# The context's rounding remainder: one instruction on GpSimd, or three on VectorE behind the pieces of the transposed remainder

## The reference

```
x: (32, 56, 160)    ctx_768: (32, 1500, 96)
x = L0(x, ctx)      attention to 3 x 16 context rows, 8 heads, w_out, + x
x = L1(x, ctx)      self-attention 20 heads of 64; cross-attention to all 1500 keys, 20 heads; GEGLU
x = L2(x, ctx)      cross-attention to 1496 keys, 8 heads, + a small attention over 4 tokens
x = L3(x, ctx)      self-attention 20 heads of 8; cross-attention to 1500 keys, 20 heads; GEGLU

cross-attention:  q = LN(x) @ wq ; k = ctx @ wk ; v = ctx @ wv
                  softmax(q k^T * scale) v ; @ wo + bo ; + x
```

## Time and profile before

| | us |
|---|---|
| median of 3 runs | 6753.15 |
| lowest, highest | 6720.8, 6789.24 |
| the profiled execution | 6721.46 |
| its span in the profile | 6719.7 |
| PE busy | 6012.4 (89%) |
| ACT, POOL, DVE busy | 3118.8 (46%), 3022.3 (45%), 2824.2 (42%) |
| mean granted clock of PE | 0.913 of full speed |

### The profile page before, as it was taken

How to read it: one execution, slowest core, us unless ns; L and a number is a source line. 1 busy time by engine, 2 the same in 40 slices (tenths; PEclk the granted TensorE clock), 3 DMA queues, 4 the chain that set the end, 5 groups by cost and what they waited for, 6 DMA issues and landing times.

```text
span 6719.7 us, 107050 instructions
## 1 busy us (share of the span) xinstructions
PE 6012.4 (89%) x34384; PEld 4911.2 (73%) x34384; DVE 2824.2 (42%) x4978; ACT 3118.8 (46%) x7280; POOL 3022.3 (45%) x2992
## 2 busy tenths in 40 slices
PE   7999999999999999998888887999989888888888
PEld 5777777777777777775666665677777777777776
DVE  2444443443433433433555544444444444444442
ACT  1444444444444444453444443345554555454554
POOL 0344444444444444452454544344554554455454
PEclk8899998898999999987999998789998999998998
DMA  2000000000000000000111111000000000000000
GB/s 54 11 14 15 10 14 15 12 14 14 14 15 8 14 14 15 11 18 19 26 27 26 25 26 29 11 18 14 14 17 18 14 14 14 15 17 14 18 14 9
DMA packets 84450, 114.90 MB, mean 17 GB/s; under 512 B 42814, under 2 KB 64682, under 8 KB 83978
## 3 DMA queue, kind: packets, MB, share of 16 engines
q1 hardware_dynamic: 83978, 108.56, 5.9%
HBM read 104.06 MB, written 4.46 MB: 16 GB/s over the span
## 4 chain that ended last, share of the span: by engine, by line
PE 66%; issue 11%; DVE 8%; ACT 7%; POOL 5%; DMA 2%; ACTq 0%; POOLq 0%; DVEq 0%; SPq 0%
PE ps_c L681 14%; PE ps_c L1061 6%; PE ps_u L1134 6%; PE ps_s L1119 5%; PE ps_s L1121 5%; PE ps_s L1120 5%; PE ps_u L1135 5%; PE ps_u L1136 5%; POOL p_lo L1587 4%; PE ps_c L1080 3%; ACT p_hi L1800 2%; ACT p L1798 1%; PE ps_c L861 1%; PE ps_c L1101 1%; PE ps_c L887 1%
## 5 line engine op out<-in xcount | busy, mean ns | idle before, releaser
L1587 POOL TENSOR_TENSOR p_lo<-p,p_hi 125x448 fp32r<-125x448 f32 (+2 forms) x2688 | 2717.8, 1021 | 3078.6 <-ACT p_hi L1800 2898.8
L1798 ACT ACTIVATE p<-ps_s 125x448 f32<-125x448 f32 (+2 forms) x2688 | 1321.1, 491 | 2330.0 <-PE ps_s L1121 2046.4
L1437 DVE TENSOR_REDUCE mpiece<-ps_c 125x1 f32<-125x500 f32 (+1 forms) x1984 | 1270.6, 672 | 320.1 <-PE ps_c L1061 301.4
L1800 ACT ACTIVATE p_hi<-ps_s 125x448 fp32r<-125x448 f32 (+2 forms) x2688 | 1315.9, 490 | 0.0
L1134 PE MATMUL ps_u<-p_hi,ctx_hi 125*97 125x448 f32 (+2 forms) x2688 | 1023.8, 381 | 171.7 <-POOL p_lo L1587 167.2
L1119 PE MATMUL ps_s<-q_hi,ctxT_hi 105*125 105x448 f32 (+3 forms) x2688 | 1023.7, 381 | 162.4 <-issue 84.9
L1120 PE MATMUL ps_s<-q_lo,ctxT_hi 96*125 96x448 f32 (+2 forms) x2688 | 951.2, 354 | 0.0
L1121 PE MATMUL ps_s<-q_hi,ctxT_lo 96*125 96x448 f32 (+2 forms) x2688 | 948.4, 353 | 0.0
L1135 PE MATMUL ps_u<-p_hi,ctx_lo 125*96 125x448 f32 (+2 forms) x2688 | 944.3, 351 | 0.0
L1136 PE MATMUL ps_u<-p_lo,ctx_hi 125*97 125x448 f32 (+2 forms) x2688 | 942.0, 350 | 0.0
L1061 PE MATMUL ps_c<-ctxT_hi,q_hi 96*125 96x500 f32 (+1 forms) x2112 | 863.1, 421 | 64.7 <-DVE mpiece L1437 23.0
(11 more groups left out here) (231 smaller groups left out, 5960.9 us busy)
## 6 DMA issues: line engine op xcount, KB each, us to landing
ctx_raw<-in_ctx SPq DMA_DIRECT2D x96, 562.5 KB
pT<-recs SPq DMA_DIRECT2D x32, 420.0 KB, 3.4
w_area<-recs SPq DMA_DIRECT2D x32, 420.0 KB, 3.4
w_area<-recs SPq DMA_DIRECT2D x32, 168.0 KB, 3.4
cs<-in_ctx SPq DMA_DIRECT2D x192, 6.0 KB, 2.8
x_between<-x_out SPq DMA_DIRECT2D x32, 80.0 KB
x_in<-x_between SPq DMA_DIRECT2D x32, 80.0 KB
w_area<-in_L_xattn_wq SPq DMA_DIRECT2D x2, 800.0 KB, 5.7
```

The lines of the kernel that those rows point to most:

```text
L1437: z = V.tensor_reduce(mpiece[0:wide, k, r:r + 1], C(0, wide, n % banks(t), 0, PIECE), AX.X, ALU.max)
L1587: P.tensor_tensor(p_lo[0:kp, k % 3, 0:w], p32[0:kp, k % 2, 0:w], p_hi[0:kp, k % 3, 0:w].bitcast(F32), ALU.subtract).then_inc(*sig("pl_ready"))
L1798: A(p32[0:kp, k % 2, 0:w], ps_s[0:kp, k % 2, 0:w], ACT.Exp, scale=DH[t.ph] ** -0.5)
L1800: A(p_hi[0:kp, k % 3, 0:w], ps_s[0:kp, k % 2, 0:w], ACT.Exp, scale=DH[t.ph] ** -0.5)\
```

## The change

`ctx_lo` is no longer made by POOL in one instruction of 1152 columns, but by DVE in three of 384 columns, each behind the piece of `ctxT_lo` of the same number. Its semaphore counts three per context instead of one, and SP and PE wait for the third. POOL's part `context` is gone.

```diff
-    "ctx_hi": ((2, 2, 2), 0), "ctx_lo": ((2, 2, 2), 1),
+    "ctx_hi": ((2, 2, 2), 0), "ctx_lo": ((6, 6, 6), 1),
...
             def load_context(t, b):
 
-                sp.wait_ge(*got("ctx_lo", t, b))
+                sp.wait_ge(*got("ctx_lo", t, NPIECE * b))
...
                         pe.wait_ge(*got("mr_ready", t, b + 1))
-                        pe.wait_ge(*got("ctx_lo", t, b + 1))
+                        pe.wait_ge(*got("ctx_lo", t, NPIECE * (b + 1)))
...
                         V.tensor_tensor(ctxT_lo[:, b, k], C(0, DC, r % banks(t), 0, PIECE), ctxT_hi[0:DC, b, k].bitcast(F32),
                                         ALU.subtract).then_inc(*sig("ctl_ready"))
+                        if r == 0:
+                            dve.wait_ge(*got("ctx_hi", t, b + 1))
+                        c = slice(4 * r, 4 * r + 4)
+                        V.tensor_tensor(ctx_lo[:, b, c, :], ctx_raw[:, 4 * DC * r:4 * DC * r + 4 * DC].rearrange("p (c d) -> p c d", c=4),
+                                        ctx_hi[:, b, c, 0:DC].bitcast(F32), ALU.subtract).then_inc(*sig("ctx_lo"))
...
-                @staticmethod
-                def context(t, b):
-
-                    yield 2
-                    pool.wait_ge(*got("ctx_hi", t, b + 1))
-                    P.tensor_tensor(ctx_lo[:, b, :, :], ctx_raw[:, :].rearrange("p (c d) -> p c d", c=NC),
-                                    ctx_hi[:, b, :, 0:DC].bitcast(F32), ALU.subtract).then_inc(*sig("ctx_lo"))
```

## The result

| | before | changed kernel |
|---|---|---|
| median, 20 runs each | 6767.64 us | 6793.76 us |
| lowest, highest | 6698.78, 6822.67 | 6768.51, 6841.44 |
| ratio to before, 95% interval | | 1.0058 (1.0035 to 1.0081) |
| span of the profiled execution, granted clock | 6719.7 us, 0.913 | 6798.1 us, 0.908 |

The ratios leave out the few runs of the kernel before that were in a slower state, and are not the quotients of the medians (here 1.0039).

A forecast was written before the change was run, and what follows sets the result against it. It took PE, busy 89% of the span, as the bound. Six places summed to 3.0 us, times 15 is +45 us; on the 6753.15 us median that gave 6798, rounded to 6795 us, range 6665 to 6880.

The forecast's parts named there:

- Sum and sign: Whole kernel: six kinds of place, 15 times each, sum to +45 us, slower, at 6795 us.
- Price of a piece: DVE's 384-column subtraction: 0.55 us bare, up to 1.7 beside a p_lo; median 0.6 to 0.9; three take 2.2 to 2.8.
- Phase 1, first, 0: First context, phase 1: POOL's wait replaced by a 0.95 us longer wait for ctxT_lo; 0 us, bounds -0.5 to +0.4.
- my own rule: On DVE: a piece that meets a running p_lo of POOL waits for its end.
- Phase 1, second, +1.7: Second context, phase 1: reciprocal 3 us late delays line 1464 and the maximum; +1.7 us, bounds 1.0 to 3.3.
- Phase 2, first, +0.4: First context, phase 2: two pieces ahead of the third correction partly fit DVE's waits for ACT; +0.4 us, between 0 and 1.1.
- Phase 2, second, +1.9: Second context, phase 2: late reciprocal carried by the DMA chain to PE in full; +1.9 us, bounds 1.0 to 3.0.
- slower rival: Second contexts: PE stalls over about 2 us before line 1061 or 1080 bring half speed; 6840 to 6928 us, chance 0.25.
- Phase 3, first, -1.8: First context, phase 3: PE's 2.24 us stall on POOL goes, some 0.4 us stays; -1.8 us, bounds -2.2 to -1.0.
- Phase 3, second, +0.8: Second context, phase 3: POOL's 1.81 us stall goes, reciprocal 2.3 us later delays line 1061; +0.8 us, bounds -1.0 to +1.8.
- POOL's row under 40 us: Changed profile's list of waits: PE's wait for POOL at line 1134, 167.2 us before, gone or under 40 us.
- faster rival: DVE absorbs the pieces in idle time: 93 us of POOL stalls and 25 of clock saved, 6635 us; chance 0.18.

The follow-up runs named there:

- e8: Against the kernel before: DVE makes the ctx_lo pieces only in first contexts of phase 3, POOL all others; 6687.14 us, ratio 0.9885.
- e12: Against the kernel before, with more rounds: DVE makes the ctx_lo pieces only in first contexts of phase 3; 6723.35 us, ratio 0.9915.
- e4: Against the changed kernel: pieces in one block behind the third ctxT_lo (first contexts) or behind the last maximum (second); 6841.90 us, 1.0103 of before.
- second profile: From running the changed kernel again, unaltered, on another chip group's rounds against the kernel before; 6832.62 us, ratio 1.0105.
- e6: Against the kernel before: nobody makes ctx_lo, it is a constant zero whose product is still formed; 6744.18 us, ratio 0.998.
- e7: Against the changed kernel: all three pieces as one block behind the third ctxT_lo, in first and second contexts; 6791.37 us, 1.0065 of before.
- e3: Against the changed kernel: in second contexts the pieces stand behind the third, fourth and fifth maximum; 6728.16 us, 0.994 of before.
- e10: Against the changed kernel: second contexts' pieces behind the third to fifth maximum, and their reciprocal earlier in DVE's queue; 6722.24 us, 0.9964 of before.
- e1: Against the kernel before: only first contexts of a pair have their ctx_lo pieces on DVE, second ones stay on POOL; 6725.76 us, ratio 0.994.
- e9: Against the changed kernel: only the reciprocal of second contexts moved earlier in DVE's queue; 6685.68 us, 0.9882 of before.

## Why the prediction was right, and where it was not

- **Sum and sign: right**, 45 us slower predicted, 26 (first comparison) and 83 us (second) measured in medians. That 6795 fell within 2 us of 6793.76 is luck: the median of before moved up by 14 us, from 6753.15 (3 runs) to 6767.64 (20 runs), the difference fell short by 19, and 3 were rounded away. By the profiles a pair takes longer by about 5 us, not 3: phase 1 second 126.6 (two profiles of the change) against 124.2 (before, e8, e12), phase 2 second 44.3 against 41.7, phase 3 second 102.8 against 99.6, phase 3 first 50.9 against 53.9, the others within 0.3. That is some 77 us for 15 pairs, in few profiles whose half-speed time varies. The sum stood near it because its errors had both signs: 1.3 us too little gain in one place, and up to 2.3 us too little loss in another.
- **Price of a piece**: least 0.539 us, as worked out from the earlier trace rows by columns. Median 0.546 in place of 0.6 to 0.9, since a little under half of the pieces met a `p_lo` (122 of 288 took over 0.7 us, up to 1.39). By the mean of 715 ns three take 2.15 us, just under my 2.2 to 2.8. The Trainium skill, "SBUF — State Buffer", section "SBUF: two separate sides", lets the later instruction wait for all of the earlier; the 1.38 us beside a running `p_lo` at 4805.39 agrees, but how often it happens is for the timeline to say.
- **Phase 1, first, 0**: +0.2 in the first profile, -0.3 in the second, by the mechanism as put: the wait for `ctxT_lo` took the place of that for POOL. By my own rule the piece that waits for the `p_lo` until 844.65 ends at 845.20, not at 844.95, which would have given +0.2.
- **Phase 1, second, +1.7**: +2.4. The reciprocal was 1.8 us late and not 3, since the pieces took 2.0 us together and not 2.8, but less was given back; in part that is half-speed time, which the term had left out.
- **Phase 2, first, +0.4**: 0.0. The pieces fit whole between DVE's waits for ACT.
- **Phase 2, second, +1.9**: +0.9 in passes without half-speed time, which is the 0.9 us that the reciprocal was late, below my bounds; +2.6 on average, because passes with half-speed time became 11 and 13 of 14 where there were 3 to 6. My slower rival had that mechanism in this very place, at 2.5 us a pass; with a cost of about 0.36 us per us at half speed (40.6 us a pass without, 44.3 with 10.2) it came to some 1.7. Its condition, a stall of over about 2 us before line 1080, was wrong: in the first profile that stall was 1.2 to 1.8 us in all 14 passes, and in e4, with 20.0 us at half speed in the mean, PE never stood there and no single wait ahead was over 0.8 us.
- **Phase 3, first, -1.8**: -3.1. The stall gave 1.5 us; the rest is the half-speed time that followed it, 7.2 us before and 3.8 after, which the term had left out.
- **Phase 3, second, +0.8: the term that was mis-sized most**, +3.1, beyond its bound of +1.8. The mechanism is the one put: the stall on POOL goes, and PE waits at line 1061 for the maximum behind the late product. The sum of the delay was wrong. From the cast to the product it was 7.63 us before (5345.50 to 5353.13) and is 11.51 now (4804.02 to 4815.53), 3.9 us later where I had 2.3. Of that 2.6 are the reciprocal (5.14 us after the cast in place of 2.54), and 1.3 the transfers: I moved the product by the reciprocal's delay alone, with phase 1's 4.93 us, and here they took 6.17 from the reciprocal's end. Over the 14 passes the broadcast landed 6.05 us after the reciprocal (5.70 in the second profile), before 4.93; in 12 (13) of them an instruction load lay beside the store, before in none. So the matmul of line 1061 that is held starts 15.4 us after the first transposes where it was 13.8, +1.6 and not +0.4. The other 1.4 us come up to the third matmul of that line behind it, where I had put 0.4; 2.9 us at half speed lie there, before none. PE's long wait there, 3.19 us, holds what POOL's stall gave back; that was in my sum.
- **Two smaller readings**: the 6.10 us from reciprocal to product of phase 2 stood in the earlier trace rows, beside the 4.93 of phase 1, so one figure for all phases was not in the rows. And two thirds of the way from +45 to -26 is 6748, not 6740.
- **POOL's row under 40 us**: wrong, 69.8. In e6, with no such instruction at all, it is still 66.1: those waits are for `p_lo`'s own time.
- **The faster rival**, 93 us of stalls won and 25 of clock, was not to be had in this order of the queues even at no cost on DVE (e6, 0.998), other than the part in first contexts of phase 3 (e12, 0.9915). Its condition was wrong: not DVE's idle time decided it, but the broadcast DMA.

Left open: why half-speed stretches come in nearly every pass of phase 2's second context in one build and in few of another. e4 and e6 have the same lengths without them (40.7 us) and the same wait of PE for POOL (66.1 us in both), and differ by 6 us a pair there. Open too: what in the program calls for the instruction load beside the store of phase 3, and how much of the 1.1 us it is; no run moves the load alone. The two stretches of the changed kernel's profile below lie in one such pass, ahead of the drop and in it (columns as in the earlier trace rows):

```profile
3844.00:3854.00 10.00, 7.86 (x52) 6.04 (x50) 4.69 (x11) 3.11 (x8) 3.58 (x3) 1.00 0.36 82
3860.00:3880.00 20.00, 19.10 (x81) 12.97 (x80) 4.47 (x13) 6.39 (x14) 4.40 (x4) 0.50 0.00 0
```

PE had 2.1 us idle in the 10 us ahead, then 20 us at half speed with almost none.

## What to carry to other kernels

A stall that goes is won only down to the next wait behind it, so that wait has to be sized in its own place: a chain of transfers that took 4.9 us in phase 1 took 6.0 in phases 2 and 3 of the changed kernel, and a consumer that never waited doesn't show what the chain will take once it is moved. Before work is moved off an engine, run the kernel without that work, and read the result place by place: here the total said that nothing was to be won, while one of six places had a gain (phase 3's first contexts, 0.9915 by themselves) that another took back. What starts a long chain of small transfers (here a reciprocal of 0.2 us) goes ahead of bulk work in its queue: its place was worth more than the whole change.

## What was not expected of the hardware

- A round trip through DRAM of some KB (store 4.4 KB, read back broadcast, 420 KB written; 1.8 and 168 KB in phase 2) took between 4.6 and 6.5 us from the end of the reciprocal to the landing in the changed kernel's profile and the one before, by what else was under way. In phase 3 the next issue came 1.4 us after the store without an instruction load beside it (all 88 passes of 14 profiles), and 2.7 in the median of the 108 passes with one.
- In phase 2 the same trip took 6.0 to 6.2 us on average where the next load of `ctx_raw` (562.5 KB) goes out 0.6 us behind the broadcast (before, the change, e6, e7), and 4.7 to 4.8 where it goes out 4 us behind it or later (e3, e4, e10). No run moves that load alone, and in phase 1 it goes out as close behind with a trip of 4.9.
- The same queues gave 122.3, 124.0, 124.6 and 125.7 us for the same contexts in four profiles (before, e1, e8, e12), with 3.1, 6.7, 7.6 and 10.6 us at half speed: one profile's clock is not the kernel's. Builds that differ in the place of a few DVE instructions had granted clocks from 0.887 (e4) to 0.913 (e7, e9, e10).
- DVE and POOL: three pieces of 0.55 us in a row took 3.44 us beside `p_lo` (e7, second contexts of phase 2), spread between other instructions 2.3 (0.81, 0.54 and 0.92 in the same place of the change). But it goes by the place and not by the row: in first contexts of phase 1 the three in a row took 1.48 us, spread 1.98, the same in all 14 passes.
